# One sampled column of three rows in four computed on TensorE instead of gathered, and a shared ring for the depthwise bands

## What is computed

```python
out = wa * gather(y0, x0) + wb * gather(y1, x0) + wc * gather(y0, x1) + wd * gather(y1, x1)
wa = (x1 - x) * (y1 - y)   # and so on
```

## Time and profile before

| | |
|---|---|
| median of 3 runs | 18490.97 us (18476.18 to 18519.87) |
| span of the profiled execution | 12341.5 us |
| the profiled execution's own time | not stated on its page |
| PE, VectorE, ScalarE, POOL busy | 63%, 42%, 13%, 71% of the span |
| mean granted TensorE clock | 0.773 of full speed |

### The profile page before, as it was taken

The page is one execution under the profiler, slowest core; times in us unless marked ns, Lnnn a source line. Parts: engine busy times, 40 slices in busy tenths (PEclk is TensorE's granted clock), DMA queues, the critical chain, the costliest instruction groups (busy, mean ns, idle before and its releaser), DMA issues.

```text
span 12341.5 us, 133270 instructions
## 1 busy us (share of the span) xinstructions
PE 7836.3 (63%) x46178; PEld 6381.1 (52%) x46178; DVE 5171.7 (42%) x6122; ACT 1646.2 (13%) x2822; POOL 8775.9 (71%) x9301
## 2 busy tenths in 40 slices
PE   5676667666467765554467765655457775655488
PEld 3555445445456644444447754444446664444474
DVE  3444444433344443443344444344344444344333
ACT  1011111110011112110001111210001111211015
POOL 4777777777777777777777777777777777777700
PEclk8787778777688877776678877776678887877689
DMA  2333333333234322332234422332224422332271
GB/s 94 100 90 101 107 88 109 109 93 100 73 126 170 118 67 82 110 96 59 71 99 163 151 69 70 102 108 71 57 81 146 171 93 64 92 115 88 62 249 56
DMA packets 878544, 1255.72 MB, mean 102 GB/s; under 512 B 183416, under 2 KB 663352, under 8 KB 860280
## 3 DMA queue, kind: packets, MB, share of 16 engines
q0 software_dynamic: 294912, 604.57, 17.4%
q1 hardware_dynamic: 512072, 596.84, 14.3%
q10 hardware_dynamic: 71344, 51.39, 1.3%
HBM read 1069.49 MB, written 245.50 MB: 107 GB/s over the span
## 4 chain that ended last, share of the span: by engine, by line
POOL 69%; issue 23%; PE 4%; DVE 1%; DMA 1%; POOLq 0%; ACT 0%; PEld 0%; SPq 0%; PEldq 0%; DVEq 0%; ACTq 0%
POOL gathered L511 69%; PE stage L1118 2%; PE stage L990 1%; PE acc L990 0%; DVE srow L1641 0%; DMA gathered<-table,idx 0%; PE pt L990 0%; DVE gathered L1634 0%; POOLq L509 0%; PE wtb L990 0%; PE acc L1260 0%; POOLq L517 0%; POOLq L507 0%; PEld acc L1260 0%; ACT room L876 0%
## 5 line engine op out<-in xcount | busy, mean ns | idle before, releaser
L511 POOL DMA_INDIRECT gathered<-table,idx x9216 | 8727.4, 947 | 2843.7 <-issue 2804.1
L1260 PE MATMUL acc<-stt,room 128*128 128x128 f32 (+1 forms) x30600 | 4374.1, 308 | 234.3 <-ACT stt L964 232.4
L1260 PEld LDWEIGHTS acc<-stt,room 128*128 128x128 f32 (+1 forms) x30600 | 4221.7, 221 | 542.9 <-ACT stt L964 339.2
L1249 PE MATMUL pt<-mat,srow 128*128 128x128 f32 x2048 | 507.8, 395 | 3644.6 <-DVE srow L1641 3644.2
L1249 PEld LDWEIGHTS pt<-mat,srow 128*128 128x128 f32 x2048 | 328.5, 197 | 3844.5 <-DVE srow L1641 3830.5
L1610 DVE COPY idx<-idxn 128x18 uint32<-128x18 uint32 x512 | 101.9, 199 | 5184.4 <-DMA gathered<-table,idx 5172.6
L1641 DVE TENSOR_REDUCE srow<-gathered 128x576 f32<-128x2304 f32 x512 | 2080.7, 4064 | 0.1
L1634 DVE TENSOR_TENSOR gathered<-gathered,wtb 128x2304 f32<-128x2304 f32 x512 | 1304.6, 2548 | 62.5 <-DMA gathered<-table,idx 62.5
L964 ACT ACTIVATE stt<-pt 128x512 f32<-128x512 f32 x512 | 305.6, 597 | 5929.2 <-PE pt L1249 5922.2
L990 PE MATMUL stage<-room,mat 128*128 128x512 f32 (+1 forms) x1360 | 796.8, 716 | 305.7 <-DVE room L1505 75.4
L1118 PE MATMUL stage<-room 128*128 128x128 f32 x7680 | 890.5, 278 | 14.1 <-DMA room<-toep 11.9
(11 more groups left out here) (211 smaller groups left out, 3940.5 us busy)
## 6 DMA issues: line engine op xcount, KB each, us to landing
gathered<-table,idx POOLq DMA_INDIRECT x9216
room<-toep SPq DMA_DIRECT2D x64, 1792.0 KB, 19.1
room<-toep SPq DMA_DIRECT2D x64, 1280.0 KB, 11.7
room<-toep SPq DMA_DIRECT2D x64, 768.0 KB, 5.0
table<-room SPq DMA_DIRECT2D x64, 512.0 KB, 2.9
toep<-in_taps SPq DMA_DIRECT2D x128, 224.0 KB
toep<-in_taps SPq DMA_DIRECT2D x128, 160.0 KB
x<-room SPq DMA_DIRECT2D x32, 512.0 KB
```

The source lines that it names most:

```text
L511: nc.gpsimd.indirect_dma_start(gat[r][:, k % K9 * G + k // K9, :], None, table[b].rearrange("(n e) -> n e", e=PAIR), bass.IndirectOffsetOn ...
L1249: ins = nc.tensor.transpose(pt[:, m, :], srow[r % 2][:, m * P:(m + 1) * P], M["ident"])
L1260: ins = nc.tensor.matmul(acc[a][:, 0:W], wk[0:kk, m, dx, block_at * C:block_at * C + P], stt[s][0:kk, m, dx:dx + W], start=start and m == ...
```

## The change

For rows 1, 2 and 3 of each step (`DENSE`), except in each image's first step, the last of the 18 sampled columns (group 1, tap 8) is not gathered. Instead:

- The 128 x 128 pixels of the group's 32 channels stay in SBUF (`img_x`), loaded once for each image by SP.
- VectorE extends the index chain by six instructions: the place (x, y) of that column goes to `hatn`, with y split into a block of 19 rows and a place in it, and with a one-of-seven selector of the block.
- ScalarE builds diagonals of x and y, TensorE spreads them over all partitions (`broadcast`), and ScalarE computes the hat in y for 20 levels (`levels`) and the hat in x (`across`).
- VectorE multiplies both (`weigh`), TensorE multiplies the 20 level matrices with the image's rows of each level (`dense`: 20 products of 7 or 6 blocks x 32 columns), and VectorE picks the block and sums (`dense` in its block) into the last 32 channels of `srow`.
- The results lie in the unused part of the bank `wtb`.

To make room, the depthwise bands of the three sizes share one ring buffer for each u (except in the last image), the stage buffers are laid out anew (`in_pairs`), `part_` is single, and the norms' and `g_in` semaphores are fewer. The depthwise stage has 13 phases instead of 10. The first step of each image is written out apart from the loop on POOL.

The core of the diff:

```diff
-ROOM = 30400
+ROOM = 21664
+DENSE = (1, 2, 3)
+ND = len(DENSE)
+ROWS_IN = 19
+BLOCKS = 7
+LEVELS = ROWS_IN + 1
...
-                        for k in range(GK):
+                        for k in range(GK - 1 if r in DENSE and not first else GK):
                             nc.gpsimd.indirect_dma_start(
...
 # SP
                 def depthwise(b, i):
-                    yield 0
                     for l in range(3):
+                        yield (0, 4, 7)[l]
                         for u in range(2):
-                            sp.wait_ge(dw_p[u], 3 * j + l + 1)
+                            sp.wait_ge(dw_p[u], 3 * j + l + (1 if b == LAST else 3))
...
                 def step(n, b, i):
                     yield 0
+                    if first_of(i):
+                        if b:
+                            sp.wait_ge(blocks_p, column(b * PER - 1, b - 1, DENSE[-1]) + 1)
+                        pairs = table[b][TABLE * PAIR:2 * TABLE * PAIR].rearrange("(x y e) -> x y e", x=W, e=PAIR)
+                        sp.dma_start(img_x, pairs[:, :, 0:CG]).then_inc(img_x_in, 16)
...
 # ScalarE
+                def diagonals(row, d):
+                    act.wait_ge(bcast_p, d)
+                    act.wait_ge(hat_s, BY_ACT * d)
+                    for c in range(2):
+                        nc.scalar.activation(hat_d[:, c, :], M["ident"], ACT.Identity, scale=hat[:, at_row, c:c + 1])
+                def levels(d):
+                    act.wait_ge(bcast_p, d + 1)
+                    nc.scalar.activation(hat_d[:, 0, :], pt[:, 0, :], ACT.Abs, scale=float(H * W), bias=neg_x)
+                    nc.scalar.activation(hat_d[:, 1, :], pt[:, 1, :], ACT.Copy, scale=float(H * W)).then_inc(hat_s, 1)
+                    for l in range(LEVELS):
+                        nc.scalar.activation(hat_u[:, l, :], hat_d[:, 1, :], ACT.Abs, bias=level_bias[l])
+                    nc.scalar.activation(hat_u, hat_u, ACT.Relu, scale=-1.0, bias=one).then_inc(hat_s, 1)
+                def across(d):
+                    nc.scalar.activation(hat_x, hat_d[:, 0, :], ACT.Relu, scale=-1.0, bias=one).then_inc(hat_s, 1)
...
+                        if r in (0, 1) and now:
+                            yield 3 * r + 1.8
+                            act.wait_ge(column_s, BY_DVE * (column(n, b, r + 2) - 1) + PICKED)
+                            across(column(n, b, r + 2))
...
 # TensorE
+                def dense(n, b, row, given):
+                    pe.wait_ge(img_x_in, 16 * (b + 1))
+                    pe.wait_ge(column_s, BY_DVE * d + WEIGHED)
+                    pe.wait_ge(weighted, v)
+                    if given:
+                        pe.wait_ge(wt_given, v + ROWS)
+                    for l in range(LEVELS):
+                        n_at = len(range(l, H, ROWS_IN))
+                        ins = nc.tensor.matmul(blocks[:, 0:n_at * CG].rearrange("p (k c) -> p k c", c=CG),
+                                               hat_a[:, l, :], img_x[:, l:H:ROWS_IN, :], start=(l == 0),
+                                               stop=(l == LEVELS - 1), skip_group_check=True)
+                    ins.then_inc(blocks_p, 1)
...
+                        if r + 1 in DENSE and now:
+                            yield 3 * r + 1.5
+                            dense(n, b, r + 1, not last_step)
                         yield 3 * r + 2
...
 # VectorE
+                def dense(n, b, row):
+                    dve.wait_ge(blocks_p, d + 1)
+                    tt(picked, blocks.rearrange("p (k c) -> p k c", c=CG),
+                       hat[:, at_row, 2:NSEL].unsqueeze(2).to_broadcast([P, BLOCKS, CG]), ALU.mult).then_inc(column_s, 1)
+                    dve.wait_ge(turned, v + 1)
+                    nc.vector.tensor_reduce(srow[row % 2][:, KC - CG:KC], picked.rearrange("p k c -> p c k"), AX.X, ALU.add)\
+                        .then_inc(column_s, 1)
+                def weigh(d):
+                    dve.wait_ge(hat_s, BY_ACT * d + ACROSS)
+                    tt(hat_a, hat_u, hat_x.unsqueeze(1).to_broadcast([P, LEVELS, W]), ALU.mult).then_inc(column_s, 1)
...
+                        if r + 1 in DENSE and now:
+                            yield 3 * r + 2.5
+                            dense(n, b, r + 1)
+                        if r in (0, 1) and now:
+                            weigh(column(n, b, r + 2))
```

More of the change, by code:

```diff
@@ L225, in build @@
         zero = sb("zero", [P, W])
+        hatc = sb("hatc", [P, 2 + LEVELS + BLOCKS + 1])
+        neg_x, one = hatc[:, 0:1], hatc[:, 1:2]
+        level_bias = [hatc[:, 2 + l:3 + l] for l in range(LEVELS)]
+        first_rows = hatc[:, 2 + LEVELS:2 + LEVELS + BLOCKS + 1]
         stats = sb("stats", [P, TB, 6])
@@ L453, in meeting, with first_of, last_of, column @@
             return meet
+        BY_ACT, SPREAD, LEVELLED, CLIPPED, ACROSS = 26, 4, 24, 25, 26
+        BY_DVE, WEIGHED, PICKED, DENSED = 3, 1, 2, 3
+        assert LEVELLED == SPREAD + LEVELS
+        def first_of(i):
+            return isinstance(i, int) and i == 0
+        def last_of(i):
+            return isinstance(i, int) and i == PER - 1
+        def column(n, b, row):
+            return ND * (n - b - 1) + DENSE.index(row)
+        def column_next(n, b, row):
+            return ND * (n - b) + DENSE.index(row)
+        def landed_by(n, b, r):
+            return 16 * (GK - 1) * (n + 1) + 16 * (b + 1) if r in DENSE else 16 * GK * (n + 1)
         def xt(t, rows=slice(0, P)):
@@ L964, in step @@
                         nc.scalar.activation(stt[r % 2][:, 0:4, 1:W + 1], pt[:], ACT.Copy).then_inc(full_ready, 1)
+                        if r == 0 and now:
+                            diagonals(3, column(n, b, 3))
+                        if r >= 2 and ahead:
+                            act.wait_ge(hat_given, n + 1)
+                            diagonals(r - 1, column_next(n, b, r - 1))
                         yield 3 * r + 3
@@ L968, in step @@
                             .then_inc(st_ready, 1)
+                        if r == 0 and now:
+                            yield 3 * r + 4
+                            levels(column(n, b, 3))
+                        if r >= 2 and ahead:
+                            yield 3 * r + 4
+                            levels(column_next(n, b, r - 1))
                 act.sem_inc(so_s, 2)
@@ L1270, in step @@
                     first = isinstance(i, int) and i == 0
+                    now, ahead = not first_of(i), not last_of(i)
+                    last_step = isinstance(n, int) and n == STEPS - 1
                     full, rest = range(MCH - 1), (MCH - 1,)
@@ L1298, in step @@
                             products(other, 3, r % 2, rest).then_inc(rows_used, 1)
+                        if r == 0 and now:
+                            broadcast(column(n, b, 3))
+                        if r >= 2 and ahead:
+                            broadcast(column_next(n, b, r - 1))
                     if isinstance(n, int) and n == STEPS - 1:
```

207 lines of the change are left out of this document (148 added, 59 removed).

## The result

| | us |
|---|---|
| before, median of its runs beside this kernel | 18498.8 |
| after, median of 4 runs (21359.3 to 21392.0) | 21384.5 |
| ratio after / before | 1.155, 95% interval 1.154 to 1.157 |
| forecast | 18055, range 17760 to 18250 |

A forecast was written before the change was run, and what follows sets the result against it. POOL's gather count was taken to bound the kernel. Gathers saved, 465 us, less 30 us kept for norm steps, took 435 us off the 18491 us median: 18056, written as 18055, range 17760 to 18250.

The forecast's parts named there:

- reading (a): Time outside the profiled span: the 6149 us between span and median lie around the span and stay; chance 0.51.
- Reading (b): Gathers on POOL: each costs 0.667 us more outside the profile, 1.918 us, so 714 us go, 17777; chance 0.27.
- POOL's instruction count sets the end: Whole kernel: POOL's gathers, 1.251 us each and 90.1 us a step, set the end; all other engines follow.
- 372 gathers are worth 465 us: POOL, three gathers fewer per step except in each image's first: 372 x 1.251 = 465 us saved.
- A row chain with 60 us of slack, under which the column is free: Other engines' row work: may lag some 60 us before POOL notices, hiding the column; 30 us kept for norm steps.
- The sizes of the operations: Column's work, per column: ScalarE 9.2 to 9.9 us, TensorE 7.4 to 8.0, VectorE's product 2.8.
- Band ring at 0, bounded by 3 us x 24: Shared depthwise band buffer: load waits hidden, 0; if the queue is late, up to 3 us in 24 steps.
- The clock in depthwise steps, over 0.95: TensorE in depthwise windows: a granted clock above 0.95 would show that the column products' price of 7.4 to 8 us holds.
- an overrun where TensorE is fullest: TensorE in heavy steps (depthwise 91, conv 92, table 88 us): 2 to 6 us over the 86.3 limit, covered by slack.
- Rival (3): Column products in TensorE's in-order queue at the 1.2 GHz price of 15 us, or slower strided reads: 18900; chance 0.08.
- Its condition: TensorE's heavy steps: the slower case decides from an overrun of 16 us a step, given as 13.5 us a column.
- The sign that the prediction named for being wrong: POOL waiting for VectorE's row sums in depthwise or norm steps, or the time outside the span moving.

The follow-up runs named there:

- e4_ring: Kernel after without the column's levels, products and picks, and with all 18 columns gathered in every row; 18812.9 us, ratio 1.017 to the kernel before.
- e1_no17: Kernel before with only the gather of column 17 left out in rows 1, 2 and 3, except in each image's first step; 18003.7 us, ratio 0.973.
- e12_skeleton: Kernel after with all hand-offs of the column kept but its large work cut to one level; 18981.5 us, ratio 1.024 to the kernel before.
- e6_keep: Kernel after with column 17 gathered as before, unused, beside the computed one; 21875.3 us, ratio 1.180 to the kernel before.
- e3_few: Kernel after with 2 of the 20 TensorE products of a column, all else kept; 20659.4 us, ratio 1.117 to the kernel before.

## Why the prediction was wrong

**The 2886 us, part by part**, in per cent of the kernel before: ring, phases and index work +1.7 (e4_ring); 372 gathers less -2.7 (e1_no17); the column's hand-offs with its small operations +3.4 (e12_skeleton's 2.4, less 1.7, plus 2.7); the column's large work +13.1 (15.5 less 2.4). The sum is +15.5 by construction, with the gathers' share taken from the kernel before; the single measurement that checks one of its terms in the kernel after is e6_keep (450 to 491 us for e1_no17's 494).

**The step that failed is the choice of reading (a).** The prediction said that the 6149 us between span and median lie around the span and stay, and made its whole sum on a profiled execution that the timed ones don't resemble. The second profile shows 1.8 us around the span, and no timed execution listed with its span has more than 2.1. The prediction had the hint in hand: by the Trainium skill, page "Runtime: NRT & Kernel Launch", section "The launch sequence", launch and end take some 9 to 15 us; the measured 1.8 us are less still, and neither leaves room for 6149. Reading (b), a dearer gather, was wrong too: a gather lasts 947 ns in both profiles, and one saved was worth 1.33 us, not 1.918. The case that was missing is the third, that all prices are as in the trace and the waits are not.

**From it follow the others.** *POOL's instruction count sets the end:* no; POOL waits 46.5 us of 136.6 in a step. *372 gathers are worth 465 us:* nearly right at 494, for another reason: gathers cost their time in series with the chain. *A row chain with 60 us of slack, under which the column is free:* this is the term that was mis-sized, 30 us for 2403 + some 640. The chain had no slack to give; it was what POOL waited for, and the column lengthens it on three engines. The sizes of the operations were partly low too: a level on ScalarE was put at 0.27 us and costs 0.30 (7440 of them, 2213 us busy; each lasts 0.387 and overlaps the next), the products of a column at 7.4 to 8.0 us and have 8.75 busy (3256.8 / 372; 7.14 for 38 of 40 records in a full stretch), the 2560-element product at 2.8 and has 2.82, the Relu at 2.3 and has 2.43. Together these are some 2 us a column, under 800 us even with nothing hidden, and could not have made 2400.

**Band ring at 0, bounded by 3 us x 24:** some 10 us a depthwise step. The largest load is itself not slower (6.9 us to landing, 19.1 in the earlier trace rows); which wait of the ring costs it was not taken apart. **The clock in depthwise steps, over 0.95:** 0.77 in a step of the kernel after:

```profile
6759.30:6916.10 156.80, 98.63 (x630) 92.67 (x630) 54.56 (x66) 39.13 (x96) 65.66 (x70) 0.77 0.27 88
```

TensorE is busy for 98.6 of 156.8 us there, not for all of it, as the forecast had it in a step of 91. Nor are the heavy steps the dear ones: the forecast sought an overrun where TensorE is fullest, but over e4_ring's a plain step grows by 23 us and a depthwise one by 3.

**The rivals.** Rival (3), "slower", put the column's products in TensorE's in-order queue at a cold price and gave 18900. The direction was right; its mechanism has a share (e3_few: 725 us for 18 products), but not its price: a column's products take 8.75 us and not 15. Most of the 2403 us comes off only when ScalarE's and VectorE's work goes too. Its condition was also mis-worked: an overrun of 16 us in a step of 86.3 leaves 36.7 us for three columns beside 35.6 and 30, so 12.2 us a column and not 13.5. The sign that the prediction named for being wrong did show: POOL waits for VectorE's row sums, 8033 us.

## What to carry over

Before a sum is made on a profile, its span must agree with the times; where it doesn't, the profile is of another kind of execution, and its waits and its slack (not its prices) are void. Where POOL issues gathers in long runs, as here, look at whether the other engines' waits end when the runs do: then, as in this kernel, work beside the gathers isn't hidden, a saved gather is worth its full pitch, and everything that lengthens the other engines' chain costs. A few microseconds without gathers, placed by hand, can be worth more than the gathers that a change saves: 6 fills after every ninth gather took 10.8% off, the change alone without its costs 2.7%.

## What the runs showed of the hardware

- Two kinds of execution of one kernel: one profile without any stall of the other engines (12341.5 us), all others with (18318.8). What decides it is open. The loads of instructions are the same in both (140 packets of 16 KB in the instruction queue), and in the second none falls in the stall from 235 to 303 us.
- What the gathers keep from the other engines is open as well. The bandwidth of the DMA engines gives no sign of it: the gathers' queue takes 13.0% of them in the profile of 18318.8 us, and more, 17.4%, in that of 12341.5, where nothing is held up.
- The Trainium skill, page "SBUF — State Buffer", section "Who interferes with whom", tells of the opposite case, VectorE locking GpSimd out so that it can't write descriptors. No run here shows that: a gather's mean is 944 to 949 ns in every run, 961 in a depthwise stretch. Here the other engines stand while POOL gathers.
- After every 18 gathers, 4.3 us without a gather took 10% off the time, and 2.9 us 0.1%; but 0.7 us after every third gather took 5% off, so this is no threshold.
